# Four attention blocks on one core: an exponential over two neighbouring banks in place of two over one bank each, with a rearranged order and prologue

## The reference

```
L0: xn = groupnorm16(x);  qkv, 8 heads of 16;  softmax(q.k / 4).v;  out = o @ w_out + b + x
L1: xn = groupnorm32(x);  qkv, 8 heads of 16;  softmax(q.k / 4).v;  out = o @ w_out + b + xn
L2: xn = layernorm(x);    q,k,v of 128 (one head);  softmax(q.k / sqrt(128)).v @ Wp + bp + x
L3: xn = groupnorm32(x);  q,k,v of 128 (one head);  softmax(q.k / sqrt(128)).v @ wp + bp + x
```

## Time and profile before

| | us |
|---|---|
| median of three runs | 2097.07 |
| the profiled execution's own time | 2098.85 |
| its span, first to last instruction | 2097.1 |
| TensorE busy with matmuls | 2034.3 (97%) |
| VectorE busy | 1676.5 (80%) |
| ScalarE busy | 1490.4 (71%) |
| GpSimd busy | 413.9 (20%) |
| mean granted TensorE clock | 0.985 |

### The profile page before, as it was taken

How to read it: one execution, slowest core, us unless ns; L and a number is a source line. 1 busy time by engine, 2 the same in 40 slices (tenths; PEclk the granted TensorE clock), 3 DMA queues, 4 the chain that set the end, 5 groups by cost and what they waited for, 6 DMA issues and landing times.

```text
span 2097.1 us, 40849 instructions
## 1 busy us (share of the span) xinstructions
PE 2034.3 (97%) x15800; PEld 1147.0 (55%) x15800; DVE 1676.5 (80%) x3104; ACT 1490.4 (71%) x2722; POOL 413.9 (20%) x544
## 2 busy tenths in 40 slices
PE   4799999999999999999999999999999999999999
PEld 3344444444744468444873448644585446846988
DVE  6799999999799978898789876898878977773433
ACT  1387788888588854988569874698747986597555
POOL 5002021220122311113120221203111031031231
PEclk7799999999999999999999999999999999999999
DMA  5401351412041314031230502305031040000000
GB/s 148 92 12 40 74 102 31 83 55 49 29 84 39 65 31 81 12 77 27 56 67 2 102 2 57 66 2 102 2 87 27 2 99 4 7 7 2 11 1 21
DMA packets 48592, 97.42 MB, mean 46 GB/s; under 512 B 7824, under 2 KB 10640, under 8 KB 48272
## 3 DMA queue, kind: packets, MB, share of 16 engines
q1 hardware_dynamic: 48400, 94.81, 21.1%
HBM read 55.98 MB, written 37.75 MB: 45 GB/s over the span
## 4 chain that ended last, share of the span: by engine, by line
PE 82%; DVE 10%; DMA 3%; ACT 2%; issue 2%; SPq 1%; POOL 1%; POOLq 0%; DVEq 0%; ACTq 0%
PE outs L1473 19%; PE banks L1435 14%; PE banks L1448 12%; PE outs L1513 11%; PE banks L1491 9%; DVE part_max L1227 8%; PE banks L1354 7%; PE banks L1360 5%; PE banks L1363 4%; ACT probs L1117 2%; DMA q_stack<-shift_parts 2%; SPq L904 0%; DMA q_scratch<-parts 0%; DVE o_turn L1239 0%; DVE stats L1166 0%
## 5 line engine op out<-in xcount | busy, mean ns | idle before, releaser
L1227 DVE TENSOR_REDUCE part_max<-banks 128x1 f32<-128x512 f32 x2048 | 1271.1, 680 | 166.6 <-PE banks L1435 161.4
L1117 ACT ACTIVATE probs<-banks 128x512 f32<-128x512 f32 x2048 | 1060.4, 611 | 200.0 <-PE banks L1448 172.8
L1473 PE MATMUL outs<-probs,v_heads 128*32 128x512 f32 (+1 forms) x5112 | 563.6, 522 | 0.8
L1435 PE MATMUL banks<-k_stack,q_stack 62*128 62x512 f32 x2048 | 550.9, 443 | 4.0 <-DVE part_max L1227 1.3
L1448 PE MATMUL banks<-q_stack,k_stack 64*128 64x512 f32 x2048 | 519.1, 444 | 21.4 <-DMA q_stack<-shift_parts 20.5
L1435 PEld LDWEIGHTS banks<-k_stack,q_stack 62*128 62x128 f32 x2048 | 257.4, 187 | 282.3 <-DVE part_max L1227 114.9
L1448 PEld LDWEIGHTS banks<-q_stack,k_stack 64*128 64x128 f32 x2048 | 244.0, 186 | 236.5 <-ACT probs L1117 77.2
L1124 ACT ACTIVATE probs<-banks,neg_max 128x1024 f32<-128x1024 f32 x128 | 142.7, 1115 | 220.9 <-DVE neg_max L1259 184.7
L1513 PEld LDWEIGHTS outs<-v_full,probs 128*128 128x128 f32 x2048 | 257.4, 191 | 47.0 <-issue 37.2
L1513 PE MATMUL outs<-v_full,probs 128*128 128x128 f32 x2048 | 276.8, 279 | 0.0
L1259 DVE TENSOR_REDUCE neg_max<-banks 128x1 f32<-128x1024 f32 x128 | 156.3, 1223 | 134.0 <-PE banks L1491 133.0
(11 more groups left out here) (107 smaller groups left out, 1160.3 us busy)
## 6 DMA issues: line engine op xcount, KB each, us to landing
k_scratch<-parts SPq DMA_DIRECT2D x64, 256.0 KB
q_scratch<-parts SPq DMA_DIRECT2D x64, 256.0 KB
k_stack<-k_scratch SPq DMA_DIRECT2D x64, 256.0 KB, 6.9
q_stack<-q_scratch SPq DMA_DIRECT2D x64, 256.0 KB, 8.2
k_stack<-k_scratch SPq DMA_DIRECT2D x64, 128.0 KB, 8.2
q_stack<-q_scratch SPq DMA_DIRECT2D x64, 128.0 KB, 9.7
q_stack<-shift_parts SPq DMA_DIRECT2D x256, 4.0 KB
tmp<-x SPq DMA_DIRECT2D x7, 512.0 KB, 3.3
```

Source lines behind the costliest of these rows:

```text
L1117: nc.scalar.activation(probs[:, plan.prob[u], 2 * n + half, :], banks[:, plan.banks["pair", t][k], :], ACT.Exp, scale=HEAD_SCALE).then_inc ...
L1227: nc.vector.tensor_reduce(part_max[:, r % 2, column:column + 1], bank_of(("tile", r, n)), AX_X, ALU.max, negate=True).then_inc(tile_max, 1)
L1435: nc.tensor.matmul(bank_of(("tile", r, n)), qs[rows, i, a, heads, P * t:P * (t + 1)], ks[rows, i, keys, heads, :], start=True, stop=True). ...
L1473: last = nc.tensor.matmul(outs[2 * HD * n:2 * HD * (n + 1), columns], v_heads[:, i, key, at:at + 2 * HD], probs[:, plan.prob[u], n, column ...
```

## The change

- A pair always takes two neighbouring banks (`take_for`); `pair` waits for both ahead of its first matmul, multiplies both halves, and only the second one signals. `exp` is one instruction of 128x1024 over both banks and all of its output. The counts in the waits (`pair_full`, `exp_done`) are halved to match.
- The order in `STEPS` is rearranged: the same tiles and pairs, 400 V and 224 U where there were 385 V and 254 U.
- In the prologue the three reads of image 1 (`k0`, `q0`, `k1`) are taken out of `first` and placed in head beats 3 and 5, so that they come behind the shift of round 0; `FIRST_STEPS` has three C fewer at its end and `STEPS` begins with `TCCCP` in place of `TPTPT`. The ones of the second half of `k_stack` are set behind the split of `q0` of image 1 and no longer behind that of `q1` of image 0.

```diff
 class Banks:
+    WHOLE_PAIRS = True
...
-        if item[0] == "pair" and part == "full":
-            (first, second), before = self.take(DOUBLES["full"], (*item, 1))
-            self.holders[first] = (*item, 0)
-            return [((first,), before), ((second,), before)]
         if item[0] == "pair":
-            return [self.take([(b,) for b in SINGLES[part]["exp"]], (*item, k)) for k in range(2)]
+            return [self.take(DOUBLES[part], item)]
...
-    FIRST_STEPS = ... "C" * 1 + "T" * 4 + "C" * 3 + "T" * 8 + "H" * 1 + "T" * 4
+    FIRST_STEPS = ... "C" * 1 + "T" * 12 + "H" * 1 + "T" * 4
-        "TPTPTTTPTUTPTU TTPTUTPTU TTPTUTPTU TTPTCUTPTU TTPTCUTPTU HTPTUTPTU TTPTPUTTU TPTPCUTTU CTPTTPTV TPTTPV "
+        "TCCCPTPTTTPTUTPTU TTPTUTPTU TTPTUTPTU TTPTCUTPTU TTPTCUTPTU HTPTUTPTU TTPTPUTTU TPTPCUTTU CTPTTPTV TPTTPV "
...
             if i == 1:
                 self.chain(h(0, 1), 0, i, ["q1"])
                 put(h(0, 2), ("write", 1, SPLIT.index("q1")))
-                put(h(0, 5), ("read", 1, "q1"))
+                put(h(0, 3), ("read", 1, "k0"), ("read", 1, "q0"))
+                put(h(0, 5), ("read", 1, "k1"), ("read", 1, "q1"))
...
-        order += [("read", 1, n) for n in ("k0", "q0", "k1")]
...
-                        if (name, layer, i) == ("q1", 0, 0):
+                        if (name, layer, i) == ("q0", 0, 1):
                             pool.wait_ge(*split_done(name, layer, i))
                             fill_ones(1)
...
-                    for k, half in enumerate(halves_of(t)):
-                        act.wait_ge(pair_full, 2 * t + k + 1)
-                        nc.scalar.activation(probs[:, plan.prob[u], 2 * n + half, :],
-                                             banks[:, plan.banks["pair", t][k], :], ACT.Exp,
-                                             scale=HEAD_SCALE).then_inc(exp_done, 1)
+                    act.wait_ge(pair_full, t + 1)
+                    first = plan.banks["pair", t][0]
+                    nc.scalar.activation(probs[:, plan.prob[u], 2 * n:2 * n + 2, :], banks[:, first:first + 2, :],
+                                         ACT.Exp, scale=HEAD_SCALE).then_inc(exp_done, 1)
...
-                    for k, half in enumerate(halves_of(t)):
+                    wait_for_banks(("pair", t))
+                    for half in halves_of(t):
                         rows = slice(ROWS * half, ROWS * (half + 1))
-                        wait_for_banks(("pair", t), k)
-                        nc.tensor.matmul(banks[:, plan.banks["pair", t][k], :], ...).then_inc(pair_full, 1)
+                        last = nc.tensor.matmul(banks[:, plan.banks["pair", t][half], :], ...)
+                    last.then_inc(pair_full, 1)
```

More of the change, by code:

```diff
@@ new lines @@
+        "PPTTTCTTTTV V CTPTTCPPPTTV PPTTV TPTPTUCCU PTTTPV TTPTTV TTPPCHTPTTCV TPTPTTTTTCV PTTUTPPTU CCPTTTV "
+        "TTPTTCCPTTV TTPTPUCCCTTTTPCCU CPTTTTTV CPCTTV HTTPTTCPTTUTPTPU TTCPCCV PTPV CCCPTPTTV CTPTTPUTTPU "
+        "CPTTPTUTTU TTPTV PTTTTV CPTHPTTTTPTTV UPTPTTU TPTTPV CPTPTTUU PTTPTV PTTPTV PTTTPUPTTU TTTPV HPTTTPPTTTTV "
+        "TTPTTV PPTTV PCTTPTV TPTPUTTCU PTPTUU TTTTPV PTTTPTTCHPTTUU TPTUTTPPU TTPV TTPPTV CCTPPTTV PTTPTUTTTTCCCCU "
+        "PCTTPTV TTPTTCCTPTCCPCTPTTV TTTPTUU HTTTTCCCCPTPPV CUCPTTCPTU PTTTCPV CPTTPTV PCTPCV PTTTTV CTTPV "
@@ new lines @@
+        "TPTTTCPTTV TPTTTCHCTPTTTV PTTV TPTTCTPTV CPPTTCUTPTTTCPTTTU PTTV CTTPTPV TPTTPV TPTTTHUPTTU PPTTV "
+        "TPTTTCTPTCV TPPTV CPPTTTV PTTPTUTPTCU TPCTUPTTTU UTPTPCPTTU HPTTV CTPTTTV PTPCTV TPTTTV PTTCPCPTTPV "
+        "TTTTTCCV TPTCCCTPTPTV TPTTTCCCTPTTUCTTPTTU PCTTHCTPCTCUTPPTTU UU TPTCCV TPTTPV CCPTTPCUU TPPTTV "
+        "TPTTPUCTPTCPTU TPTTV HTPPTTTTTPTTV TTPV TTTPV TTPPV CPTTTPV TPTPTTV TTPTPUTTPU TTPTPV TPTHUTPTU TPTTTV "
+        "PPTTV TTPTTPUU CPTTPUU TPTTPCV TPTTPV TPTTPUTTPU TPTCTPTTTV PPV PTTTV TTHSV CTTSR CSCR GGGTTTTTTGGGR "
@@ new lines @@
+        "TTPPV TTPV TTHSV CSR CTTCR GTTTTTTTGGSGSGSGR GGYR R SSGGGGGGTTTTTTCGCGCYR TTTTGGGSGCCGCGTTTTGGR SCYCSGR "
+        "GGCTTTTGCGGR TTTTGHGCR YSGGCSGGCCR SGTTTTTGGGCCYR SCGGR GGGTTTTGSSGGYR TTCTCGGR GGTTTTPGGGGYTTR "
+        "CPTTTGGGGGGTTPTTGGPPYTTCUTTPTTU V PTTTTCHCPPTTCCPPTTTV V PTTPV PTTTTCV TPTTPV TPPTTUU CPTPTTV PTTPTV PTTPTV "
+        "PTPTTV CHPTTPV TTTPPV TTPTTTTCPCUU PPTTV CPTTPTV PTTPCUU PTPTTV PTTTPV PTTPTV TPPTTV CHTPPCTTV TTTPPV "
+        "CTPPTTV TPTTPCV TPPTTUCU PTTPTV PTTPTV TPTTPV PTTTPV PTTPV CPTTTTCUPTTU HPTTCUPPTTCCCU CTTPTTV "
@@ L875, in read @@
                     if g >= 2:
[L876 removed]
+                        sp.wait_ge(pair_full, 2 * STAGE_SLOTS * (g - 1))
                     for c in range(first, first + 2):
@@ L1340, in wait_for_banks @@
                         elif before[0] == "pair":
-                            pe.wait_ge(exp_done, 2 * before[1] + before[2] + 1)
+                            pe.wait_ge(exp_done, before[1] + 1)
                         elif before[0] == "scores":
@@ L1444, in pair @@
                         pe.wait_ge(shift_in[r % 2], 16 * SHIFTS * (r // 2 + 1))
-                    for k, half in enumerate(halves_of(t)):
+                    wait_for_banks(("pair", t))
+                    for half in halves_of(t):
                         rows = slice(ROWS * half, ROWS * (half + 1))
-                        wait_for_banks(("pair", t), k)
-                        nc.tensor.matmul(banks[:, plan.banks["pair", t][k], :],
-                                         ks[rows, i, key // QT, first + n, P * (key % QT):P * (key % QT + 1)],
-                                         qs[rows, i, a, first + n, :], start=True, stop=True).then_inc(pair_full, 1)
+                        last = nc.tensor.matmul(banks[:, plan.banks["pair", t][half], :],
+                                                ks[rows, i, key // QT, first + n, P * (key % QT):P * (key % QT + 1)],
+                                                qs[rows, i, a, first + n, :], start=True, stop=True)
+                    last.then_inc(pair_full, 1)
                 def wait_for_outs(before):
```

93 lines of the change are left out of this document (39 added, 54 removed).

## The result

| | us |
|---|---|
| before, median of five runs beside it | 2095.68 (2089.77 to 2097.71) |
| after, median of five runs | 2105.23 (2102.41 to 2108.11) |
| ratio, 95% interval | 1.0048 [1.0033, 1.0064] |
| profiled execution of after, its span | 2105.23, 2103.4 |

What follows compares the result with a forecast made beforehand. TensorE was taken to bound the kernel, with VectorE's row maxima setting the pace from 100 to 500 us. −10.4 − 2.1 − 4.7 + 7 = −10.2 us gave 2087 us, range 2069 to 2104.

Steps and rivals of the forecast that it cites:

- the slower case: Head rounds: pairs wait for their younger bank, tiles queue behind, VectorE and ScalarE run dry; +21.5 us, 2119; chance 0.16.
- prologue: Before the first pair: moving memsets and image 1's reads away shortens two TensorE holes; −10.4 us, bounds −12 and −4.
- order, U and V: TensorE's values: 15 pairs of U become V, each saving 0.141 us; −2.1 us.
- banks: Pair loads: neighbouring banks come back later and are wanted earlier; +7 us, a fifth of 34, bounds 0 and 34.
- ScalarE: Exponentials: one of 1024 replaces two of 512, saving 119 us of ScalarE's time; −4.7 us overall, bounds −25 and +20.
- My measure of a bank's age: Bank pool: a pair's younger bank was last used 6.0 matmuls ago on average, in place of 7.
- Nothing else changes in TensorE's own work: TensorE: side-by-side slots stay nearly equal, 2185 against 2183, so only U and V change its work.
- first hole: Prologue, TensorE waiting for bias work: moving GpSimd's memsets starts the first tile 4.0 us earlier; 3.5 kept, bounds 0 and 4.7.
- the two holes: Prologue: two 12.13 us gaps before TensorE, one ended by bias work, one by the landing of round 0's shift.
- The tell-tale: From the first pair on: same time, up to 10 us more or less; 15 off means pairs and banks are mispriced.
- a smaller sign than I asked for: Pair weight-load waits: far above 153 us, with VectorE and ScalarE idle longer, would show the neighbouring banks making it slower.

Runs made afterwards that it cites:

- e1: Kernel before with only the new prologue: image 1's reads behind round 0's shift, ones set later, three C moved forward; 0.9918 of before, 2081.59 us.
- e2: e1 with the changed kernel's order, pairs as before (single banks, a wait for each, two exponentials of 512); 0.9980 of before.
- e4: Changed kernel with two exponentials of 512 per pair, each starting on its own bank, banks still waited for and released together; 1.0090 of before.
- e11: e2 with neighbouring banks, a wait for each bank ahead of its own matmul, two exponentials each releasing its own; 1.0046 of before.
- e9: e1, but TensorE may reuse either bank of a pair only when both exponentials are done; 1.0147 of before.
- e12: Changed kernel, but each of a pair's two matmuls waits for its own bank only; banks, order and single exponential stay; 1.0000 of before.
- e5: e1, but a pair waits for both of its singly taken banks ahead of its first matmul; 0.9995 of before.
- e6: e1 with neighbouring banks for each pair, older first, waits and releases kept apart, two exponentials; 1.0177 of before.
- e10: e1, but both exponentials of a pair start only when both banks are full, each bank released by its own; 0.9991 of before.
- e3: Changed kernel with e1's order: neighbouring banks and one exponential of 1024 per pair; 1.0392 of before.
- e8: e1 with the ones set where they were before, so only the reads are moved; 0.9963 of before.

## Why the prediction was wrong

The mechanism was named, as the slower case: neighbouring banks come back too late. Its size in the sum was wrong, and the order had a price that the sum left out. The steps, in the forecast's own terms, with differences of ratios times 2097 us (each good to 5 to 9 us; they add up to the whole by the way they are taken, e1, e2, e4, after):

| step | forecast | measured | from |
|---|---|---|---|
| prologue | −10.4 | −17 | e1 |
| order, U and V | −2.1 | +13 | e2 − e1 |
| banks | +7 | +23 | e4 − e2 (14 of it e11 − e2) |
| ScalarE | −4.7 | −9 | after − e4 |
| sum | −10.2 | +10 | |

Of the 20 us between forecast and result, 16 lie in the banks and 15 in the order; the prologue and ScalarE gave 11 more than forecast.

**The banks: the first step that failed.** The forecast counted 140 pairs at one slot of 0.24 us and took a fifth. Three things in it were wrong. First, the unit: what a late bank waits for is the end of an exponential, and the jumps in e9 reach that far (0.52 us), two slots and not one. Second, the cover: I let most waits vanish behind the matmul still running. e9 shows that little slack was there. In the trace of before, from 100 to 500 us, 38% of the banks that pairs take are refilled within 0.5 us of the end of the instruction that read them (median 0.62; for tiles 0.55). In after it is 67%, median 0.38. The wait rows don't show this, for they count what was late and not what was nearly late. Third, the release: a pair now gives both its banks back at one time, which stood in no term and costs 48 us by itself on the old order. On the new order the 23 us are 14 for the choice of neighbours and 9 for the common wait and release; the common wait by itself is 10 by e12, so within the error nothing is left for the release there. My measure of a bank's age could not have told any of this: by the same count the younger bank of a pair was last used 5.9 matmuls ago on the old order and 6.0 on the new one, and neighbours cost 54 us on the one and 14 on the other. The bounds (0 and 34) held the value, and the slower case's +34 was nearer than my +7.

**The order: the second step that failed.** Values took 425.5 and 135.0 us, where I expected 428 and 136, and all the same e2 is 13 us slower than e1. I compared the counts of the letters and not their places. "Nothing else changes in TensorE's own work" is wrong: after has 330 matmuls fewer than before (15470, 15800), and values are only 120 of them (4992, 5112). The other 210 are products of projections: `product` cuts one that stands beside values in the order into four strips of 32 columns. With the new order 74 projections of q, k and v are cut where 90 are in e1. In e1's trace a whole q or k projection between tiles and pairs takes 1.06 us to the next start (median of 20) and a cut one ahead of values 0.88 (of 28); values ahead of a cut one take 0.88 and not 1.00. An estimate from these rows is 0.17 to 0.29 us for each of the 16, 3 to 5 of the 13 us. What the rest is was not settled. Much of it is lost by round 16, where e2's trace stands at −2.8 and e1's at −13.3, but the traced execution of e2 is 7 us longer than its median.

On the order before, each single change of wait, choice, start or release costs 15 to 54 us (e5, e6, e9, e10). They overlap, for one by one they come to 133 us, and everything together, with the cheaper exponential, to 99 (e3). The new order bears neighbours (14 us in place of 54) and pays 13 us with single banks. Which property of an order makes it so was not tested.

**ScalarE.** The exponential of 1024 takes 1023 ns alone, between the copy (1012) and the form with bias (1115). The saving is 1060.4 − 1001.7 = 59 us of its time and not 119: I took off 94 ns of overlap for each, as if the wide ones stood in a row, but they take 978 ns each on average. The time fell by 9 us (after − e4, good to some 6) where 4.7 were forecast, within the bounds. The Trainium skill, "ScalarE: Activation LUTs", section "What ACT_TABLE_LOAD costs", would have 1039 ns; the trace has 1023. Its 93 ns of overlap is for neighbours back to back, and here 488 of the 1024 start after the instruction before them has ended.

**The prologue.** Its mechanism was right, and so was the time of the first pair; over the whole the step gave 17 us (good to some 6), beyond its bound of 12. The bias products start at 30.46 (31 forecast), the first tile at 40.55 (40), the first pair at 67.28 (68), after 1.85 us idle; the four copies take 0.62 us. Image 1's reads behind the shift make the parts land 3.9 us after readiness, not 12.2. e1's first pair is 12.35 us earlier than before's, its median 17 us.

The other 5 us (6.3 in the two traces) lie behind the first pair, and the traces show where they may be. Before waits 8.4 us for four later landings of the shift, e1 6.2 for three. And behind most such holes the granted clock is lower for a while. These rows of before are a hole, the values behind it at the lower level of the clock (1.2 GHz, 0.50 in the window's row) and the next ones at the higher (2.4 GHz):

```profile
1459.46 0.50 PE L1448 MATMUL banks<-q_stack,k_stack 64*128 64x512 f32 x2 [2.33 <-DMA q_stack<-shift_parts]
1460.62 1.93 PE L1473 MATMUL outs<-probs,v_heads 128*32 128x512 f32 x8
1463.88 1.04 PE L1473 MATMUL outs<-probs,v_heads 128*32 128x512 f32 x8
```
```profile
1460.00:1463.40 3.40, 3.40 (x16) 1.01 (x14) 2.03 (x4) 2.09 (x5) 0.00 (x0) 0.50 0.00 0
```

Behind its first pair before has 22.4 us at the lower level (to 87.8, and four stretches of 3.4 us, three of them after such holes), e1 13.3 (to 73.1, and two). At half the speed these 9 us are worth up to 4.6, as an estimate; with the 2.2 us of holes that would cover the difference, but no kernel tested it. It fits the other executions: the mean granted clock of before is 0.986 and of e1 0.990, and among the executions of before alone those at 0.983 took 2101 us or more and those at 0.989 took 2086 to 2091. The kernels from e1 on stand at 0.989 to 0.991, so the clock weighs less in the differences between them; e8 alone stands at 0.988, which may be why it is 9 us behind e1 and its first pair only 4.9.

One bound was summed wrong, without effect: no advance in the first hole and the old 7.6 us of landing leave 79.02 − (66.83 + 2.72 + 7.6) = 1.9 us of gain, not 4.6. e8 parts the two holes: with only the reads moved, the first pair is 7.4 us earlier, and moving the ones brings 4.9 more.

**The tell-tale.** "15 less or more from the first pair on" came out as 18.0 more, and the price of the banks was wrong, as that sentence said. The pair loads' waits rose from 153 to 201 us, a smaller sign than I asked for. The windows show the place better: VectorE's work from 100 to 500 us fell by 7.8 us. Since e1 takes 2011.8 us from its first pair on (2078.5 − 66.67), 6 less than before, banks and order together cost 24 us there and not 18.

One exponential over two banks that are no neighbours, which would keep the choice of single banks, was not tried; nor was an order written for own waits with wide exponentials (e12).

## What to carry to other kernels

Here the order had slack only for the way of taking banks that it was written for. Before changing how buffers are taken or given back, measure for each reuse the time from the reader's end to the refill, and count how many of these are shorter than the delay. This count at a whole reader instruction each is an upper bound and no price: in e1's trace a third of the pairs' first banks are refilled within 0.52 us, which would be some 180 us, and e9 measured 48. A wider instruction saves overhead on its own engine but holds all its buffers to its end and starts only at the last input: on the old order these two cost 48 and 15 us by themselves, and the wide exponential 41 net over 820 pairs. Take a change that bundles parts apart on the chip; here one part alone (−17 us) beats the whole.

## What the runs showed of the hardware

- GpSimd's memset slows some VectorE work and not other. Two `tensor_scalar` of 128x128 take 2.88 us beside it and 0.29 without, four copies 3.94 and 0.62. In before the two `tensor_scalar` end at 31.43 and 31.49, just after the first memset (31.34), and the first two copies at 35.02 and 35.09, just after the second (34.94). The 32 row maxima of 512 from PSUM from 41.35 on in after take 19.21 us, 0.600 each, against 0.602 before; one by one the 13 that overlap the memsets take 671 ns, all 32 take 675. By the rule of the Trainium skill, "SBUF — State Buffer", section "Who interferes with whom", both were to be expected: the lock lasts a whole instruction, and `tensor_reduce` does not contend. The trace agrees.
- Late banks don't show in an average of TensorE: it is busy 97% in before, in after and 98% in e1, with 27 us between the last two. The same 15794 matmuls are busy 2031.5 us in e1, 2067.4 in e9 and 2084.2 in e3, so part of what they wait stands in the trace as busy time. VectorE's busy time in a window of the stretch that it paces was the better gauge (386.5 us in e1, 379.9 in after, 365.0 in e3).
- Holes in front of TensorE came with a lower clock behind them. In before those that end at 215.99, 1206.84 and 1459.46 (1.97, 3.63 and 2.33 us) are each followed by 3.4 us at a granted clock of 0.50; behind the last two, eight matmuls of values take 1.93 us there and not 1.04.
